# First attention of a four-layer kernel: where the items of a two-bank ring and one reduction per step stand in the order of work

## The reference, cut to what matters

```python
q, k, v = (proj(Wq), proj(Wk), proj(Wv))              # x: (16, 256, 128)
a_q, a_k, a_v = Eq[rel], Ek[rel], Ev[rel]             # rel = clip(l - m, -64, 64) + 64
logits = (content(q, k) + rel_k(q, a_k) + rel_q(k, a_q) + pos_pos(a_q, a_k)) * scale
attn = softmax(logits)
out = einsum('bhlm,bhmd->bhld', attn, v) + einsum('bhlm,lmd->bhld', attn, a_v)
x = layernorm(x + out)
```

## Time and profile before

| | us |
|---|---|
| runs of the kernel (three) | 5007.28, 5020.37, 5029.31 |
| median | 5020.37 |
| the profiled execution: time | 5004.04 |
| the profiled execution: span | 5002.2 |
| a step of the first attention | 55.6 to 56.7 |

### The profile page before, as it was taken

One profiled execution on the slowest core, in us unless ns is written; L12 is line 12 of the kernel. 1 busy time (PEld: TensorE's weight loads), 2 busy tenths in 40 slices (PEclk: granted clock), 3 DMA queues, 4 the chain that ended last, 5 costly groups with the idle time before them and its releaser, 6 DMA issues. The chain is left out here.

```text
span 5002.2 us, 202509 instructions
## 1 busy us (share of the span) xinstructions
PE 4560.0 (91%) x82160; PEld 3754.4 (75%) x82160; DVE 3696.6 (74%) x7406; ACT 3399.6 (68%) x6468; POOL 3558.5 (71%) x2507
## 2 busy tenths in 40 slices
PE   6888888799999999999999999999999997888879
PEld 4777777678887888788877887888877885555557
DVE  4877777788887888778877888788877884555544
ACT  3565565577777777777777777777777774666664
POOL 3334334499999999989999999999999995222212
PEclk8999999999999999999999999999999998999889
DMA  4333333332223222332223222322232221000000
GB/s 119 98 101 112 98 104 105 93 84 69 68 69 88 70 68 69 73 83 69 69 72 85 70 69 70 87 69 70 68 74 70 69 68 40 1 0 0 0 1 18
DMA packets 500471, 338.98 MB, mean 68 GB/s; under 512 B 222559, under 2 KB 489084, under 8 KB 499213
## 3 DMA queue, kind: packets, MB, share of 16 engines
q1 hardware_dynamic: 493566, 320.55, 25.3%
q10 hardware_dynamic: 6544, 13.18, 0.9%
HBM read 60.06 MB, written 54.58 MB: 23 GB/s over the span
## 5 line engine op out<-in xcount | busy, mean ns | idle before, releaser
L1420 POOL TENSOR_TENSOR b_rnorm<-b_ss,neghalf 128x16 f32<-128x16 f32 x384 | 1118.2, 2912 | 25.1 <-DVE b_ss L1956 21.5
L1416 POOL TENSOR_TENSOR b_rot<-b_t 128x1024 f32<-128x1024 f32 x384 | 909.5, 2369 | 75.3 <-DVE b_t L1945 74.6
L1943 DVE TENSOR_TENSOR b_t<-psum,b_cosg 128x1024 f32<-128x1024 f32 x384 | 469.6, 1223 | 426.3 <-ACT b_sq L1798 420.3
L1427 POOL TENSOR_TENSOR b_qk<-b_rot,b_rnorm 128x1024 f32<-128x1024 f32 x384 | 731.0, 1904 | 42.8 <-POOL b_rnorm L1420 2.7
L1544 PE MATMUL psum<-b_w_hi,b_xT_parts 128*128 128x512 f32 x1152 | 528.0, 458 | 28.6 <-issue 19.3
L1798 ACT ACTIVATE b_sq<-psum 128x1024 f32<-128x1024 f32 x384 | 392.1, 1021 | 221.9 <-PE psum L1549 221.5
L1950 DVE TENSOR_REDUCE b_ss_floor<-b_sq 128x16 f32<-128x1024 f32 x384 | 464.3, 1209 | 0.0
L1549 PE MATMUL psum<-b_w_hi,b_xT_parts 128*128 128x512 f32 x1152 | 459.9, 399 | 0.0
L1545 PE MATMUL psum<-b_w_lo,b_xT_parts 128*128 128x512 f32 x1152 | 457.3, 397 | 0.0
L1631 PE MATMUL psum<-shared,b_oT 128*128 128x128 f32 x3072 | 425.2, 281 | 0.8 <-ACT b_oT L1816 0.8
L1533 PE MATMUL psum<-ident,b_qk 128*128 128x128 f32 x3072 | 405.9, 275 | 21.3 <-DVE b_o L1982 15.3
(11 more groups left out here) (271 smaller groups left out, 11545.8 us busy)
## 6 DMA issues: line engine op xcount, KB each, us to landing
b_v_win<-b_v SPq DMA_DIRECT2D x2304, 65.0 KB
keyed<-shared SPq DMA_DIRECT2D x64, 768.0 KB, 4.7
b_v_win<-b_v SPq DMA_DIRECT2D x1152, 32.5 KB
a_logits<-keyed SPq DMA_DIRECT2D x128, 160.0 KB, 3.1
oa<-XR SPq DMA_DIRECT2D x1024, 2.0 KB
xcur<-X SPq DMA_DIRECT2D x111, 128.0 KB, 4.3
shared<-in_L_ffn_Wqkv_dram ACTq DMA_DIRECT2D x6, 1536.0 KB
a_logits<-keyed SPq DMA_DIRECT2D x64, 128.0 KB, 3.0
```

The source lines that it names most:

```text
L1416: nc.gpsimd.tensor_tensor(rot[:, i, :, :], t1[:, i, :, :], t2[:, i, :, :], ALU.add).then_inc(rot_done, 1)
L1420: nc.gpsimd.tensor_tensor(rnorm[:, i, :], ss[:, i, :], neghalf[:, :], ALU.pow).then_inc(rn_done, 1)
L1427: nc.gpsimd.tensor_tensor(qk[:, i, :, :], rot[:, i, :, :], rnorm[:, i, :, None].broadcast_to((P, 16, BD)), ALU.mult).then_inc(qk_done, 1)
L1943: nc.vector.tensor_tensor(t14, x4, tab(cosg, slice(0, BD), BD), ALU.mult)
```

## The change

Four things are reordered; no instruction is added or taken away.

- The second query block of each half (qe(0,1), qe(1,1)) is no longer set by TensorE as four items in a row behind the second turn. Its first item now stands between the two items of outputs(0) (or outputs(2)), its second behind them, its third and fourth behind the first two parts of the next scores. The first block is set two items behind each turn. The items of `ks` move into scores(2), behind its third and fourth part, and `v` before the second turn of group 1. kb 4 and 5 stand behind the third and fourth part of scores(0).
- The ring's order follows, so both y(0) items are in one bank, and both y(2) items.
- ScalarE's copies follow the same order, some of them between the two halves of `exps` or behind them.
- VectorE: `sums(g)` moves from directly behind `outputs(g)` to behind the next group's additions, low parts and key masks, just ahead of `maxima(g + 1)`; `ln_statistics` moves ahead of `outputs(0)`.

```diff
@@ -454,8 +454,9 @@
             qs, ks = [("qs", 0), ("qs", 1)], [("ks", 0), ("ks", 1)]
 
             orders = {"first": ["x"] + qs + qe(0, 0) + qe(0, 1) + ks + ["v"] + kb + qe(1, 0) + qe(1, 1),
-                      "loop": (["x"] + qs + qe(0, 0) + qe(0, 1) + y(0) + ks + ["v"] + y(1) + kb[:4]
-                               + qe(1, 0) + qe(1, 1) + y(2) + kb[4:] + y(3)),
+                      "loop": (["x"] + qs + qe(0, 0) + y(0)[:1] + qe(0, 1)[:1] + y(0)[1:] + qe(0, 1)[1:] + ks + ["v"]
+                               + y(1) + kb[:4] + qe(1, 0) + y(2)[:1] + qe(1, 1)[:1] + y(2)[1:] + qe(1, 1)[1:]
+                               + kb[4:] + y(3)),
                       "last": y(0) + y(1) + y(2) + y(3)}
             ring_fill, ring_fills = ring_plan(orders, 2)
             ring = bank[0:2]
@@ -633,10 +634,16 @@
                                     if i == 1:
                                         out_of("x")
                                     project_groups(qs[i - 1:i], wq_rep)
+                                if g == 2 and i < 2:
+                                    keyed_queries(qe(0, 1)[2 + i:3 + i])
+                                if g == 2 and i >= 2:
+                                    project_groups(ks[i - 2:i - 1], wk_rep)
                                 if g == 3:
                                     spread_block(kb[i])
                                 if g == 0 and i < 2:
-                                    spread_block(kb[4 + i])
+                                    keyed_queries(qe(1, 1)[2 + i:3 + i])
+                                if g == 0 and i >= 2:
+                                    spread_block(kb[2 + i])
 
                             o = [score[:, kq, :].rearrange("p (h m) -> p h m", h=8) for kq in range(4)]
 
@@ -678,14 +685,15 @@
                                                                       mt * P:(mt + 1) * P], ident[:, :])
                                 last.then_inc(turn_full, 1)
 
-                        def outputs(g):
+                        def outputs(g, part=range(2)):
 
                             pe.wait_ge(turn_out, b * 16 + 4 * g + 4)
                             lt, hh = g // 2, g % 2
 
                             if g == 0:
                                 pe.wait_ge(values_ok, LT * b + LT)
-                            for n, name in enumerate(y(g)):
+                            for n in part:
+                                name = y(g)[n]
                                 r, full = room(name)
                                 for j in range(4):
                                     for mt in range(LT):
@@ -719,32 +727,34 @@
                             scores(0, 0)
                             return
                         ahead = part == "loop"
+
+                        def turns_and_outputs(g):
+
+                            turn(g, 0)
+                            if ahead:
+                                keyed_queries(qe(g // 2, 0)[:2])
+                            turn(g, 1)
+                            if ahead:
+                                keyed_queries(qe(g // 2, 0)[2:])
+                            outputs(g, (0,))
+                            if ahead:
+                                keyed_queries(qe(g // 2, 1)[:1])
+                            outputs(g, (1,))
+                            if ahead:
+                                keyed_queries(qe(g // 2, 1)[1:2])
+
                         if ahead:
                             turn_x()
                         scores(1, b)
-                        turn(0, 0)
-                        if ahead:
-                            keyed_queries(qe(0, 0))
-                        turn(0, 1)
-                        if ahead:
-                            keyed_queries(qe(0, 1))
-                        outputs(0)
+                        turns_and_outputs(0)
                         scores(2, b)
                         turn(1, 0)
                         if ahead:
-                            project_groups(ks, wk_rep)
+                            project_v()
                         turn(1, 1)
-                        if ahead:
-                            project_v()
                         outputs(1)
                         scores(3, b)
-                        turn(2, 0)
-                        if ahead:
-                            keyed_queries(qe(1, 0))
-                        turn(2, 1)
-                        if ahead:
-                            keyed_queries(qe(1, 1))
-                        outputs(2)
+                        turns_and_outputs(2)
                         if ahead:
                             for name in kb[2:4]:
                                 out_of(name)
@@ -808,13 +818,13 @@
                                 nc.scalar.copy(probsT[:, mt, :, half, :, :],
                                                turned[mt].rearrange("p (h w l) -> p w h l", h=4, l=HD)).then_inc(turn_out, 1)
 
-                        def keyed_queries(lt, f):
+                        def keyed_queries(lt, f, part_of=slice(0, 4)):
 
                             seq = 0 if part == "first" else b + 1
-                            if lt or not isinstance(seq, int) or seq > 0:
+                            if part_of.start == 0 and (lt or not isinstance(seq, int) or seq > 0):
                                 act.wait_ge(keyed_wr[f], 16 * (2 * seq + lt))
                                 act.wait_ge(far_ok, 4 * seq + 2 * lt + f - 1)
-                            for name in qe(lt, f):
+                            for name in qe(lt, f)[part_of]:
                                 r, free = take(name)
                                 nc.scalar.copy(keyed[:, 2 * name[2]:2 * name[2] + 2, :],
                                                r[:, 0:2 * KJ].rearrange("p (h j) -> p h j", h=2)
@@ -839,20 +849,24 @@
                             high_parts(qs, q_next)
                         turns(0, 0)
                         if ahead:
-                            keyed_queries(0, 0)
+                            keyed_queries(0, 0, slice(0, 2))
                         turns(0, 1)
                         if ahead:
-                            keyed_queries(0, 1)
+                            keyed_queries(0, 0, slice(2, 4))
+                            keyed_queries(0, 1, slice(0, 1))
                         exps(1, 0, b)
+                        if ahead:
+                            keyed_queries(0, 1, slice(1, 2))
                         exps(1, 1, b)
+                        if ahead:
+                            keyed_queries(0, 1, slice(2, 4))
+                            high_parts(ks, k_parts)
                         turns(1, 0)
                         if ahead:
-                            high_parts(ks, k_parts)
-                        turns(1, 1)
-                        if ahead:
 
                             act.wait_ge(values_ok, LT * b + LT)
                             projected_v()
+                        turns(1, 1)
                         if norm:
                             ln_normalise(act, b - 2)
                         exps(2, 0, b)
@@ -863,14 +877,19 @@
                             load_projections()
                         turns(2, 0)
                         if ahead:
-                            keyed_queries(1, 0)
+                            keyed_queries(1, 0, slice(0, 2))
                         turns(2, 1)
                         if ahead:
-                            keyed_queries(1, 1)
+                            keyed_queries(1, 0, slice(2, 4))
+                            keyed_queries(1, 1, slice(0, 1))
                         exps(3, 0, b)
+                        if ahead:
+                            keyed_queries(1, 1, slice(1, 2))
                         exps(3, 1, b)
                         if not ahead:
                             load_output_projection()
+                        else:
+                            keyed_queries(1, 1, slice(2, 4))
                         turns(3, 0)
                         turns(3, 1)
                         if ahead:
@@ -990,17 +1009,18 @@
                             low_parts(qs, q_next, q_low)
                         add_keyed(1, b, 1)
                         maxima(1, b)
-                        outputs(0)
-                        sums(0)
                         if norm:
                             ln_statistics(dve, b - 2)
+                        outputs(0)
                         add_keyed(2, b, 0)
+                        if ahead:
+                            low_parts(ks[:1], k_parts, k_low)
                         add_keyed(2, b, 1)
                         if ahead:
-                            low_parts(ks, k_parts, k_low)
+                            low_parts(ks[1:], k_parts, k_low)
+                        sums(0)
                         maxima(2, b)
                         outputs(1)
-                        sums(1)
                         if ahead:
```

(11 more changed lines are left out.)

## The result

The changed kernel took 5070.12 us (median of 4 runs, 5064.62 to 5086.14), the kernel before beside it 5019.01 us (4 runs). The ratio is 1.0108, with a 95% interval of 1.0076 to 1.0140: slower by 51 us by the medians, 54 by that ratio. The forecast was 5062 in a range of 5030 to 5088. The profiled execution took 5072.0 us (span 5070.2), 68 us more than that of before; of these 68, about 16 belong to before's execution, which lay that far under its median.

The account below looks back on a forecast made before the run. TensorE, in order, was taken to carry the step, its turn hanging on VectorE. A step of 51.7 + 6.5 = 58.2 us against 55.65 gave 14 x 2.6 = 36, plus 7: +43 us, so 5062, range 5030 to 5088.

Parts of the forecast that it names:

- Its walk: The new order laid out in time from one x to the next: kb 7 at 51.7, step 58.2 against 55.65.
- The end of the step: From kb 7 to next x: sums(2) ahead of maxima(0) adds 2.3 us, making 4.20 into 6.5.
- Waits exchanged inside the step: From x to kb 7: every removed wait matched by one for a mask behind a reduction, 51.7 against 51.45 us.
- The blocked multiplication: VectorE's small multiplication ahead of kb 0: held again until GpSimd's second k_diag operation ends, at 30.0 us.
- The bound of +1.2: Upper margin per step, if copies come later or VectorE's small operations are held at other places: +1.2 us.
- The other bound, -0.7: Lower margin per step, without the blocked small multiplication on VectorE: 0.7 us less.
- The clock: TensorE's granted clock: read as granted in full before the change; no term for a fall.
- Loop step 0, the tail, the rest: Steps cost 2.6 us each, last loop step and tail 7 together; the other three layers only start later.
- The sum: Whole kernel: fourteen steps at 2.6 give 36 us, last loop step and tail 7, together +43 us.
- The first: Rival: the waits go and none replaces them; a step loses 4 to 5 us, 4953 in all; chance 0.06.
- The second: Rival: a draw, walk pessimistic inside, kb 7 at 50; step +0.6 or less, 5020 to 5040; chance 0.18.
- The third: Rival: SyncE's queue of stores becomes the bound; step of 60, +65 us, 5085 to 5100; chance 0.08.

Follow-up runs that it names:

- experiment 5: Changed kernel with sums(2) and sums(0) back directly behind their outputs: 5002.31 us against 5015.69 for the kernel before, ratio 0.9974.
- experiment 1: Changed kernel with only sums(2) back directly behind outputs(2): 5048.34 us against 5013.3 for the kernel before, ratio 1.0073.
- experiment 10: Kernel before with sums(2) alone moved, behind the masks of kb and ahead of maxima(0): 5066.3 us, ratio 1.0103.
- experiment 6: Changed kernel with useless transposes filling both long TensorE holes, 30 ahead of x and 26 ahead of kb 0: 5063.17 us, ratio 1.0099.
- experiment 3: Changed kernel with VectorE's old order; ring, TensorE and ScalarE as changed: 5011.14 us, ratio 0.9994 to the kernel before.
- experiment 8: Changed kernel with sums(0) and sums(2) back, sums(1) behind maxima(3), statistics between the two masks of outputs(0): 4996.02 us, ratio 0.9957.
- experiment 9: experiment 8's kernel with the load of x ahead of the stores of group 1 on SyncE: 4976.36 us, ratio 0.9929.
- experiment 12: experiment 9's kernel with a GpSimd wait added, so k_diag starts behind VectorE's maxima(2): 4981.55 us, ratio 0.9936.
- experiment 11: experiment 7's kernel with a GpSimd wait added, so k_diag starts behind VectorE's maxima(2): 5002.05 us, ratio 0.9974.
- experiment 7: Kernel before with two VectorE moves, statistics ahead of outputs(0) and sums(1) behind maxima(3): 5022.28 us, ratio 1.0015.

## Why the prediction held, and where it was off

One chain of undisturbed steps at clock 1.00 says what each part does: 55.65 before; 53.40 with all but sums(0) and sums(2) (experiment 5), -2.25; 55.85 with sums(0) (experiment 1), +2.45; 58.50 with sums(2), +2.65. The forecast had 58.2.

Its walk against the step that starts at 864.05, in us behind x:

| | forecast | measured |
|---|---|---|
| y(0), first item | 10.6 | 10.51 |
| y(0), second item | 13.5 | 13.66 |
| scores(2) | 15.45 | 15.74 |
| y(1) | 25.3 | 25.27 |
| kb 0 | 30.7 | 31.35 |
| turn(2, 0) | 35.2 | 35.79 |
| y(2), second item | 42.6 | 42.86 |
| turn(3, 0) | 49.5 | 49.48 |
| kb 7 | 51.7 | 51.66 |
| next x | 58.2 | 58.50 |

- *The end of the step: right.* Forecast 6.5 from kb 7 to x, measured 6.84; the 0.34 are about what the small multiplication lost to GpSimd's copies (0.58 for 0.17). Experiments 1 and 10 show the cause, 2.65 and 2.65 to 2.85, for the 2.3 of the sum and that multiplication.
- *Waits exchanged inside the step: right as a sum, incomplete as a reading.* The waits came where the walk put them. But I read them as one package, in which statistics, sums(0) and the ring's order cancel, and did not price the parts apart. Experiment 5 shows a gain of 2.25 beside a loss of 2.45. The walk's own numbers had it: kb 0 would have come 2.3 earlier without sums(0) in front of maxima(2).
- *The blocked multiplication: right in kind, wrong in the operation.* I expected maxima(2)'s to end with GpSimd's second k_diag operation. It ran free at 716.65 in the changed kernel; sums(0)'s was held instead, 1.12 for 0.22, with 0.6 more at kb 0 than the walk had. The bound of +1.2 for small operations held at other places, or late copies, covered it. The other bound, -0.7 for a free multiplication, was too large: 30.0 against 29.4 and its own 0.17 leave 0.4.
- *The clock: the term that was missing.* The sum took all work at the clock of the earlier trace rows, 1.00. The holes that it forecast, 3 and 2.7 us, cost another 1 us a step through the clock (59.47 against 58.50; 56.82 against 55.85 in experiment 1; experiment 6). With twelve of the thirteen steps hit, that alone is as much as the 10 us by which they exceed the forecast.
- *The first step: a term that was missing.* Taken as unchanged, it was 6.1 longer, by the banks and a lower clock (experiment 3).
- *Loop step 0, the tail, the rest.* 4.0 instead of 2.6; 8.3 instead of 7 for the last two. The stage's last stores in SyncE's timeline, then VectorE's last multiplication (columns as in the earlier trace rows):

```profile
1002.35 23.26 SPq L187 DMA_DIRECT2D oa<-XR  x48
```

```profile
1025.63 0.23 DVE L996 TENSOR_TENSOR XR<-a_ysum,a_rsum 128x64 f32<-128x64 f32 x1
```

  The 48 stores end at 1025.6, 63 us later than in the earlier trace rows, and the multiplication comes 62 later. What follows the stage was 5.6 longer, against nothing in the sum. No kernel here changes anything behind the stage, and from the stage's last multiplication to the end the fourteen profiled executions took 4038 to 4055 us, so 5.6 lies within that spread.
- *The sum.* 43 forecast, 68 measured between the profiled executions: 10 more from the thirteen steps, 6 from the first, 2.7 from loop step 0 and the tail, 5.6 from the rest. The total came out 8 us off and not 25: I carried the 16 us between before's profiled execution and its median over to the changed kernel, whose profiled execution lay 2 us above its own median. By medians the change costs 51 us. So part of the nearness is luck.
- *The rivals.* The first (no wait takes the place) is out: three did. The second (a draw) would have needed kb 7 at 50; it came at 51.66. The third (stores) did not decide here, and showed itself in experiments 8, 9 and 12, as a mechanism of steps under 54 us. The forecast had 51 us for SyncE's round; there it took 54.

## What to carry to other kernels

Before a reduction is moved "out of the way", look at what stands right behind its new place: work that only frees a buffer can be put in front of anything with slack, but not in front of the operation for which the next step's first item waits. Price the parts of a reordering apart, since a gain of 2 us and a loss of 2.5 us in the same step look like nothing. And a hole of 3 us in an engine with a throttled clock can cost more than its length: here about every second one brought a slow stretch that cost 1 us, so count that in.

## What the hardware showed that I had not expected

- TensorE's granted clock fell to 0.50 for 3.4 us at a time, in a stage where TensorE was busy 48 of 59 us: 13 falls in thirteen steps, 1 in experiment 3, whose longest wait in an undisturbed step is 1.0. Ten stand at single idle stretches of 2.7 to 3.4 us, three at two shorter ones in a row (1.9 and 0.7 twice, 1.2 and 1.4); 13 of the 23 long stretches brought none.
- A running operation of GpSimd held VectorE's smallest operations on SBUF until its end: 0.17 became 0.57, 0.94 and 1.45, and 0.22 became 1.12. One wait on GpSimd's side (experiment 11) removed that of maxima(2), for 1.2 us a step or more. Reductions with one operand in SBUF were not held.
- TensorE shows holes for which the trace has no releaser, at the same instructions of the outputs and scores. In the kernel before they are at most 1.2 us, with one of 4.8; in the changed kernel up to 1.9, with one of 3.4; in experiments 5 and 7 several are of 2.8 to 4.2. One in TensorE's timeline of experiment 5:

```profile
743.61 0.23 PE L708 MATMUL psum<-a_v_far,a_probsT 128*32 128x36 f32 x2 [2.81 <-issue]
```

  They take a part of the gain (mean 54.73 for undisturbed 53.40 in experiment 5), but they don't simply grow as steps get shorter. Their sum over the thirteen steps is 8.6 us before, 11.2 in the changed kernel, 6.5 in experiment 3, 15.6 in experiment 5, 24.5 and 25.4 in experiments 7 and 11, and only 6.7 and 8.9 in experiments 9 and 12, the fastest. One of them keeps its place whatever the order: in thirteen of the fourteen kernels a hole of 3.3 to 4.8 us stands at the end of the seventh of the thirteen steps, ahead of x (or of the transposes that fill the hole there). Their cause stays open; no run was aimed at them.
